# Row sums of the first layer's attention: a two-part reciprocal, spread by float32r products on 128 rows

## The reference

```python
scores = jnp.einsum('bhtd,bhsd->bhts', q, k) / jnp.sqrt(jnp.float32(Dh))
scores = jnp.where(causal, scores, -jnp.inf)
probs = jax.nn.softmax(scores, axis=-1)
out = jnp.einsum('bhts,bhsd->bhtd', probs, v)
out = out.transpose(0, 2, 1, 3).reshape(b, t, d)
return out @ w_out.T + b_out
```

## Time and profile before

| what | value |
|---|---|
| median of 3 runs | 2471.0 us (2461.97 to 2471.63) |
| profiled execution, span from first to last instruction | 2475.1 us |
| profiled execution, own whole time | not listed beside its span |
| share of the span: PE, DVE, ACT, POOL busy | 94%, 74%, 52%, 42% |
| first layer's passes that hold the edit | about 98 to 770 us |

### The profile page before, as it was taken

How to read it: one execution, slowest core, us unless ns; L and a number is a source line. 1 busy time by engine, 2 the same in 40 slices (tenths; PEclk the granted TensorE clock), 3 DMA queues, 4 the chain that set the end, 5 groups by cost and what they waited for, 6 DMA issues and landing times.

```text
span 2475.1 us, 55054 instructions
## 1 busy us (share of the span) xinstructions
PE 2335.6 (94%) x19136; PEld 2091.7 (85%) x19136; DVE 1840.2 (74%) x5136; ACT 1276.7 (52%) x3807; POOL 1039.9 (42%) x1090
## 2 busy tenths in 40 slices
PE   4899999999997799999999999889999999999999
PEld 3677887878876678888888887789999999999999
DVE  5777777777777766666666665568878888888876
ACT  2666566665654355555555555424325555555522
POOL 4545545446453545545545545123332222222063
PEclk7899999999998999999999999999999999999999
DMA  4321211211220221221122122132116777777444
GB/s 114 107 52 46 56 38 51 54 46 47 47 86 10 63 55 44 50 56 46 47 56 50 47 52 69 43 69 43 39 30 234 236 233 240 232 228 240 149 118 126
DMA packets 153080, 225.73 MB, mean 91 GB/s; under 512 B 54294, under 2 KB 123174, under 8 KB 142054
## 3 DMA queue, kind: packets, MB, share of 16 engines
q1 hardware_dynamic: 143942, 203.56, 28.6%
q0 software_dynamic: 8864, 18.66, 2.9%
HBM read 159.32 MB, written 27.16 MB: 75 GB/s over the span
## 4 chain that ended last, share of the span: by engine, by line
PE 69%; DVE 13%; POOL 7%; issue 5%; ACT 5%; DMA 1%; POOLq 0%; SPq 0%; DVEq 0%; ACTq 0%
PE bank L55 54%; PE bank L136 7%; PE bank L340 2%; POOL P L1743 2%; PE bank L367 2%; PE bank L1253 2%; PE bank L1293 1%; ACT Ph L622 1%; DVE xe L885 1%; ACT PTh L634 1%; POOL Qn L1768 1%; POOL Qn L1766 1%; DVE tb L1606 1%; POOL xr_lo L1775 1%; DVE Ph L771 1%
## 5 line engine op out<-in xcount | busy, mean ns | idle before, releaser
L1447 ACT ACTIVATE P<-P,mx 128x144 f32<-128x144 f32 x512 | 206.2, 405 | 264.1 <-DVE mx L1568 263.2
L2579 POOL DMA_INDIRECT xE<-d_y,ixs x78 | 112.5, 1442 | 336.0 <-PE bank L136 305.8
L55 PE MATMUL bank<-xD_hi,w1e_lo 128*128 128x256 f32 x880 | 251.1, 285 | 0.0
L55 PE MATMUL bank<-w2e_hi,hrD_hi 128*128 128x256 f32 x880 | 249.0, 283 | 0.0
L55 PE MATMUL bank<-w2e_lo,hrD_hi 128*128 128x256 f32 x880 | 248.9, 283 | 0.0
L55 PE MATMUL bank<-w2e_hi,hrD_lo 128*128 128x256 f32 x880 | 248.9, 283 | 0.0
L1743 POOL TENSOR_TENSOR P<-P,rs 128x512 f32<-128x512 f32 x128 | 133.3, 1042 | 273.8 <-DVE rs L1577 270.3
L1079 POOL TENSOR_TENSOR xe<-xe 128x704 f32<-128x704 f32 (+3 forms) x64 | 88.4, 1381 | 376.0 <-DVE xe L890 375.8
L55 PE MATMUL bank<-xD_lo,w1e_hi 128*128 128x256 f32 x880 | 245.9, 279 | 0.0
L55 PE MATMUL bank<-xD_hi,w1e_hi 128*128 128x256 f32 x880 | 245.6, 279 | 0.0
L2188 ACT ACTIVATE hD<-bank,b1E 128x256 f32<-128x256 f32 x312 | 127.0, 473 | 197.2 <-PE bank L55 182.8
(11 more groups left out here) (324 smaller groups left out, 8005.1 us busy)
## 6 DMA issues: line engine op xcount, KB each, us to landing
w1raw<-in_ew SPq DMA_DIRECT2D x39, 1024.0 KB, 5.7
w2raw<-in_ew SPq DMA_DIRECT2D x39, 1024.0 KB, 4.9
K<-Kn SPq DMA_DIRECT2D x256, 72.0 KB, 2.1
Q<-Qn SPq DMA_DIRECT2D x256, 64.0 KB, 2.0
d_ys<-oE SPq DMA_DIRECT2D x39, 256.0 KB, 2.7
d_rot<-QK SPq DMA_DIRECT2D x16, 512.0 KB, 2.9
Rs<-d_rot SPq DMA_DIRECT2D x64, 128.0 KB, 4.4
b2E<-in_eb SPq DMA_DIRECT2D x39, 128.0 KB, 3.6
```

Source lines behind the costliest of these rows:

```text
L55: inst = e.matmul(out, l, r, start=k == 0, stop=k == len(pairs) - 1)
L1447: inst = e.activation(P1[t % 2][:, n, :], P1[t % 2][:, n, :], ACT.Exp, bias=mx1[t % 2][:, 2 * g + sg:2 * g + sg + 1], scale=-1.0, accum_ou ...
L2579: e.indirect_dma_start(out=xE[q % 2][c], out_offset=None, in_=d_y, in_offset=bass.IndirectOffsetOnAxis(ap=ixs[r % 4][:, c:c + 1].bitcast(U ...
```

## The change

`invert_sums` still takes the reciprocal, and then writes it in two parts to a new tile `rsp` (128 by 2 by 128, float32r): in columns 0 to 15 of each half the rounded value, in columns 16 to 31 the rest, in the others the zeros that POOL set at the start. For that it has two more DVE instructions and waits between them, and a new wait, since `rsp` is one buffer. `turn_sums` turns all 128 columns, `sums_copy` copies 128 rows to `rsT`, which is float32r now, and `spread_sums` multiplies all 128 rows by `sel0r`, a float32r copy of `sel0` whose rows 16 to 31 repeat rows 0 to 15, so that both parts are added. ACT makes that copy at the start, and the load of `sel0` has 128 rows.

```diff
-        w_out0, rsT, OT0 = tile("w_out0", 2, 256), tile("rsT", 256), tile("OT0", 2, 256)
+        w_out0, rsT, OT0 = tile("w_out0", 2, 256), tile("rsT", 256, dt=F32R), tile("OT0", 2, 256)
...
+        rsp, sel0r = tile("rsp", 2, 128, dt=F32R), tile("sel0r", 2, 128, dt=F32R)
...
-            for dst, src in ((raw0, "w_qkv0"), (b_qk0, "b_qk0"), (rot0, "rot0k"), (sel0[0:16], "sel0"),
+            for dst, src in ((raw0, "w_qkv0"), (b_qk0, "b_qk0"), (rot0, "rot0k"), (sel0, "sel0"),
...
-                turn(e, [(banks[6][0:16, st * 128:st * 128 + 128], rs0[b % 2][:, st, :]) for st in range(2)]
+                turn(e, [(banks[6][:, st * 128:st * 128 + 128], rsp[:, st, :].bitcast(F32)) for st in range(2)]
                      ).then_inc(p_rsT, 1)
...
-                    inst = e.matmul(halves(7)[:, G, :], sel0[0:16, G, :], rsT[0:16, :], start=True, stop=True)
+                    inst = e.matmul(halves(7)[:, G, :], sel0r[:, G, :], rsT, start=True, stop=True)
                 inst.then_inc(p_bc, 1)
...
-                e.activation(rsT[0:16, :], banks[6][0:16, 0:256], ACT.Copy).then_inc(c_rsT, 1)
+                e.activation(rsT, banks[6][:, 0:256], ACT.Copy).then_inc(c_rsT, 1)
...
                 e.wait_ge(l_wa, 16 * 8)
+                e.activation(sel0r, sel0, ACT.Copy)
...
                 e.wait_ge(c_P, 16 * (b + 1))
-                e.reciprocal(rs0[b % 2], rs0[b % 2]).then_inc(v_ri, 1)
+                if b:
+                    e.wait_ge(p_rsT, b)
+                else:
+                    e.wait_ge(g_V, 2)
+                inv, hi, lo = rs0[b % 2], rsp[:, :, 0:16], rsp[:, :, 16:32]
+                e.reciprocal(inv, inv).then_inc(*vs.up())
+                e.wait_ge(s_v, vs.n)
+                e.tensor_copy(hi, inv).then_inc(*vs.up())
+                e.wait_ge(s_v, vs.n)
+                e.tensor_tensor(lo, inv, hi.bitcast(F32), ALU.subtract).then_inc(v_ri, 1)
...
             e.wait_ge(s_const, 1)
+            e.memset(rsp.bitcast(F32), 0.0)
...
-    sel = np.zeros((16, 2, 128), np.float32)
+    sel = np.zeros((128, 2, 128), np.float32)
     for r in range(256):
-        sel[rows[r] // 16, r // 128, r % 128] = 1.0
+        sel[rows[r] // 16::16, r // 128, r % 128][0:2] = 1.0
```

## The result

The changed kernel takes 2484.0 us, the median of 5 runs (2480.02 to 2490.49), against 2471.63 us (5 runs, 2461.97 to 2472.78) of the kernel before: +12.4 us between the medians. The ratio, taken over all runs, is 1.0056 with a 95% interval of 1.0036 to 1.0075 (the two medians alone give 1.0050). That is outside the forecast range (2464 to 2482) and slower by just over 0.5%, which had a chance of 0.08. The profiled execution took 2490.49 us, the slowest of the five, with a span of 2488.7, 13.6 us more than the span before; what is read from it is that execution's, not the median's.

The account below looks back on a forecast made before the run. The prediction took DVE's chain ahead of the turn and ACT's run behind it to bound each pass, not PE. Full passes +3.6, run-out −0.5, start +0.3 gave +3.4 us on 2471.0: 2474.4 us, range 2464 to 2482.

Parts of the forecast that it names:

- DVE's `invert_sums`: Ahead of the turn of the sums: added copy, subtraction and handover delay the turn by 0.44 us a pass.
- Turn of the sums: PE's two transposes, ahead of `first_values`: loading 128 weight columns in place of 16 costs 0.05 us a pass.
- The spread saves 0.9, both gaps go: PE's spread products behind `first_values`: 0.9 us less PE time a pass, without the loader's two 0.33 us gaps.
- ACT's run is the floor and gives 0.21: Between `first_values` and `values`: ACT's unbroken work sets the time; only its gap ahead of `hidden_high` closes, 0.21 us.
- The wait at `values` grows to 1.4: PE, arriving earlier at `values`, waits there for ACT: 1.4 us in place of 0.69.
- A pass of 45.07 us: One full pass over a batch of the first layer was to take about 45.07 us, from 44.8.
- The sum of +3.4 us: Whole kernel: full passes +3.6, run-out −0.5, ramp 0 and start +0.3 us, total +3.4.
- 13 passes at +0.28: The 13 full passes of the first layer, each +0.28 us net (+0.44 + 0.05 − 0.21), together +3.6.
- the unseen: Chance of 0.04 left for anything that no forecast term or rival covered.
- The ramp 0: The one pass in the ramp at the start: no change, somewhere between −0.5 and +0.44 us.
- Rival 1: PE decides and keeps the spread's saving: −0.4 us a pass, 2465.5 us in all; chance 0.13.
- Rivals 2 and 3: DVE's added operations at shared-stretch price, 2491 us, chance 0.05; or at their lower bound, 2471.8 us, chance 0.12.

Follow-up runs that it names:

- e1: Kernel before the change, with only DVE's two-part inverse added; PE still turns and spreads 16 rows in fp32: 1.0026 of the kernel before.
- e10: Kernel before the change, with ACT's `exps` ahead of `x1_high` and DVE's `invert_sums` at step 6, ahead of `gated`: 0.9988 of the kernel before.
- e7: Changed kernel, with ACT's `exps` ahead of `x1_high` and DVE's `invert_sums` at step 6, ahead of `gated`: 0.9953 of the kernel before.
- e9: Changed kernel, with one reciprocal and the 128-row spread in fp32 in place of float32r: 2486.18 us (one run), kernel before beside it 2483.98.
- e6: Changed kernel, with ACT's `exps` of step 0 put ahead of `x1_high`: 0.9986 of the kernel before.
- e3: Changed kernel, with eight more float32r products, read by nobody, in PE's idle time ahead of a pass's first `values`: 1.0012 of the kernel before.
- the repeat: The changed kernel run and profiled again, with nothing altered: 2488.69 us, 1.0056 of the kernel before.
- e2: Changed kernel, with one reciprocal straight into columns 0 to 15 of `rsp`, the rest part left zero: 0.9994 of the kernel before.
- e4: Changed kernel, with DVE's `invert_sums` moved from step 7 to step 6, ahead of `gated`: 0.9990 of the kernel before.
- e5: Changed kernel, with `invert_sums` at step 6 and eight unread float32r products ahead of a pass's first `values`: 0.9991 of the kernel before.
- e8: Kernel before the change, with only ACT's `exps` put ahead of `x1_high`: 1.0002 of the kernel before.

## Why the prediction was wrong

Step by step, as it was put:

- *DVE's `invert_sums`: 0.71 us in place of 0.27, +0.44.* Measured 0.71, with the copy at 0.18, the subtraction at 0.19 and the handovers as taken. Beyond it the first instruction of `hidden_steps` behind it lasts 0.88 in place of 0.83 us, so the turn comes 0.49 later (e1: the pass grows by 0.49). The Trainium skill's table (VectorE: DVE Perf Modes, the TRN2 errata) gave an estimated 77 and 94 ns for the two; the trace has 180 and 190 ns, which speaks against the table and agrees with the longer fixed part that the same section reports.
- *Turn of the sums, +0.05.* From the turn to `x1_high` it is 2.18 us in place of 2.15: +0.03.
- *The spread saves 0.9, both gaps go.* The loads show 0.35 in place of 1.05 us and no gap, and T to `values` shrinks by 0.93 where nothing hides it (e10 to e7). Right. The Trainium skill's rule on changes of tiling mode (TensorEngine Tiling (Array Packing), Key Properties), on which the prediction drew, agrees with e9: 128 rows without the change of format have no gap either.
- *ACT's run is the floor and gives 0.21.* Measured 5.44 to 5.22 us, −0.22; that ACT's run is the floor is shown by e6 and e7, where another order of ACT moves `values`.
- *The wait at `values` grows to 1.4.* 1.41 to 1.44.
- *A pass of 45.07 us.* The seven passes without a fall take 45.06 to 45.08, e3 45.09. The sum of +3.4 us is what e3 measured for the kernel in which the hole is filled (+4.0 on the medians).
- *13 passes at +0.28.* **This is the step that failed.** The prediction took every pass behind the edit to be as before and the longer idle time of PE to cost nothing. In 5 of the 12 full passes (4 in the repeat, 2 in each of e2 and e4) the granted clock goes to 0.50 behind the hole, and those passes take 1.5 to 1.6 us longer. That is 7.8 us in the first profile and 6.2 in the repeat. Of the 13 passes that the prediction counts, six fall in the first profile, the thirteenth (44.94 us, against 43.45 in the repeat) among them. No term of the sum stood for it, and the chance of 0.04 for the unseen was all that it had.
- *The ramp 0.* +3.6 in the first profile, +0.3 in the repeat; the difference is one more fall behind `values` (clock 0.54 from 109 to 116 us), so the same step failed here. With it and the thirteenth pass the falls make some 12.6 of the 13.6 us of the first profile (7.8 + 1.5 + 3.3, the last two against the repeat). The medians, which don't hang on one profile, have +12.4 and +13.9.

What is shown, for the full passes: the fall goes with the longer hole. It is there with the hole and without the later turn (e2, e4), and gone when the hole is filled (e3, e5), shortened (e6, e7, e9) or never grown (e1, e8, e10). Holes of 1.41 to 1.44 us brought 13 falls in 48 full passes (four profiles), holes up to 0.80 none in 108 (nine profiles, the one of before among them). No length between 0.80 and 1.41 was tried in a full pass. What stays open: why one pass falls and its neighbour doesn't with the same hole; whether idle time at the turn raises the rate (9 of 24 full passes with it, 4 of 24 without, too few to tell); and how many falls the unprofiled runs have, since they give only a mean clock (0.975 to 0.977 in the changed kernel's other four runs, 0.970 in the profiled one). In the repeat four falls × 1.56 are 6.2 us, the passes 3.4 and the ramp 0.3, together 9.9; its profiled execution lies 10.4 us above the median of the kernel before (2485.25 against 2474.8). The other 3.4 us of its +13.9 are between this execution and the median of its five, and no profile shows them. Rival 1 (the saving is kept) was wrong as the kernel stands; in e7, with both orders changed, the saving is kept. Rivals 2 and 3 were wrong, since the DVE term was the one forecast.

## What to carry to other kernels

A saving on the engine that is 94% busy becomes idle time if another engine's run is the floor in that place; work out how long that idle time gets, and treat a hole of PE that grows, as here from 0.69 to 1.4 us, as a possible cost, with the granted clock per pass as the thing to look at. Then look for what makes the floor: here one reordering on DVE and one on ACT turned the same change from 1.0056 to 0.9953 of the kernel before, while the same reorderings without it gave 0.9988. And compare passes one by one: the mean of 45.72 us hid two kinds, 45.07 and 46.63.

## What the runs showed of the hardware

Where PE was busy for 1.59 of 3.00 us, with an idle stretch of 1.41 in it, the granted clock could drop to 0.50 for the next 3 us, in a pass of 45 us of which PE is idle for some 2.3 (42.80 busy of 45.10). In the ramp's pass, where PE is busy less (41.81 of 45.84 us in the repeat), it did so behind a hole of 1.16 us in four of seven profiles. float32r products of 256 columns started 0.12 us apart at the full clock and 0.21 apart at the lower one. The Trainium skill, TensorE: Matmul & The Clock Gate, A second HAM failure mode, tells of a kernel in which short idle times between groups of products make the clock go back and forth between its two levels; the trace agrees with that, with a fall in 5 of 12 passes. A change from 128-row to 16-row products and back cost a gap of 0.33 us of the loader on each side; with 128 rows throughout there was none, in float32r or in fp32.
